# A recurrent layer, a banded attention and a routed FFN in one launch: layer norms by rows, and the router's mask by replacing the two largest logits

## The reference, cut to what matters

```python
h = tok(x)                         # 16 sequences, 375 rows of 128; z, f, o from a 2-tap convolution,
                                   # c = f*c + (1-f)*z along the rows, h = o*c: 374 rows of 128
h = h + attention(layernorm(h))    # 8 heads; each row looks back at 33 near offsets (0..32)
                                   # and at 48, 64, 96, 128, 192, 256; gated; then W_out, b_out
h = h + ffn(layernorm(h))          # logits over 64 experts, top 2, softmax weights,
                                   # at most 128 rows per expert, one shared GELU FFN (512 wide)
def layernorm(x): return (x - mean(x)) / sqrt(var(x) + 1e-5)    # over the 128 channels of a row
```

## Time and profile before

| | |
|---|---|
| median of 3 runs | 496.3 us (495.8 to 497.25) |
| the profiled execution's own time | 499.14 us |
| its span, first to last instruction | 497.3 us |
| mean granted clock of TensorE | 0.991 of full |
| h of sequence 0 and of sequence 15 made at (L831) | 11.3 and 405.3 us |

### The profile page before, as it was taken

One profiled execution on the slowest core, in us unless ns is written; L12 is line 12 of the kernel. 1 busy time (PEld: TensorE's weight loads), 2 busy tenths in 40 slices (PEclk: granted clock), 3 DMA queues, 4 the chain that ended last, 5 costly groups with the idle time before them and its releaser, 6 DMA issues.

```text
span 497.3 us, 12720 instructions
## 1 busy us (share of the span) xinstructions
PE 473.4 (95%) x4698; PEld 298.6 (60%) x4698; DVE 404.3 (81%) x837; ACT 303.0 (61%) x539; POOL 396.5 (80%) x444
## 2 busy tenths in 40 slices
PE   7689799999999999999999999999999999999994
PEld 5334446465665666666566556656655666658673
DVE  3678797888888898888789788888978889878764
ACT  4456566665765756566475657657555665747664
POOL 6299989997987879698878969878796988986511
PEclk9799999999999999999999999999999999999999
DMA  6000539080724417081542707145180633535901
GB/s 246 15 1 1 132 62 190 11 181 2 180 28 115 94 58 150 2 192 16 129 79 57 151 1 181 27 112 97 52 157 1 164 45 94 100 96 97 192 18 31
DMA packets 54222, 44.27 MB, mean 89 GB/s; under 512 B 27248, under 2 KB 41488, under 8 KB 54032
## 3 DMA queue, kind: packets, MB, share of 16 engines
q1 hardware_dynamic: 54160, 43.45, 39.5%
HBM read 24.59 MB, written 18.85 MB: 87 GB/s over the span
## 4 chain that ended last, share of the span: by engine, by line
PE 79%; DVE 6%; POOL 5%; issue 4%; DMA 4%; ACT 2%; SPq 1%; POOLq 0%; DVEq 0%; ACTq 0%
PE bank L367 19%; PE bank L353 8%; PE bank L462 7%; PE bank L485 6%; PE bank L332 6%; PE bank L333 5%; PE bank L430 4%; PE bank L417 3%; PE bank L341 2%; PE bank L346 2%; PE bank L409 2%; PE bank L381 2%; PE bank L437 2%; PE bank L442 2%; PE bank L447 2%
## 5 line engine op out<-in xcount | busy, mean ns | idle before, releaser
L1140 POOL TENSOR_TENSOR prod<-q,k 128x1496 f32<-128x1496 f32 x48 | 144.0, 3014 | 13.3 <-ACT q L630 13.3
L850 DVE SCALAR_TENSOR_TENSOR prod<-bank,par,k 128x1496 f32<-128x1496 f32 x80 | 139.5, 1768 | 7.5 <-ACT q L630 7.5
L1182 POOL TENSOR_TENSOR acc<-acc,tmp 128x310 f32<-128x310 f32 (+4 forms) x80 | 64.8, 810 | 38.4 <-DVE tmp L907 24.1
L367 PE MATMUL bank<-prod,ew 128*32 128x374 f32 x1024 | 90.3, 481 | 0.8 <-DVE mixin L817 0.8
L1125 POOL TENSOR_TENSOR fprod<-q,k 128x374 f32<-128x374 f32 (+6 forms) x112 | 80.2, 746 | 0.0
L654 ACT ACTIVATE scT<-bank 128x374 f32<-128x374 f32 x48 | 23.2, 484 | 64.8 <-PE bank L367 64.8
L353 PE MATMUL bank<-xn,par 128*128 128x374 f32 x128 | 53.7, 506 | 2.9 <-DVE xn L839 2.9
L485 PEld LDWEIGHTS bank<-par,hid 128*128 128x128 f32 x384 | 47.6, 191 | 9.9 <-issue 6.8
L367 PEld LDWEIGHTS bank<-prod,ew 128*32 128x32 f32 x1024 | 28.9, 110 | 37.6 <-issue 34.7
L485 PE MATMUL bank<-par,hid 128*128 128x128 f32 x384 | 50.1, 275 | 0.9 <-ACT hid L713 0.9
L907 DVE TENSOR_TENSOR tmp<-bank,vT 128x310 f32<-128x310 f32 (+4 forms) x80 | 30.3, 380 | 23.9 <-PE bank L409 22.2
(11 more groups left out here) (130 smaller groups left out, 977.4 us busy)
## 6 DMA issues: line engine op xcount, KB each, us to landing
band_scratch<-attn SPq DMA_DIRECT2D x16, 769.5 KB, 6.0
band<-band_scratch SPq DMA_DIRECT2D x64, 192.0 KB, 3.8
v<-v_scratch SPq DMA_DIRECT2D x32, 192.0 KB, 5.0
v_scratch<-vtok SPq DMA_DIRECT2D x16, 192.0 KB, 4.1
xT<-x_dram SPq DMA_DIRECT2D x16, 187.5 KB, 4.2
out_dram<-osb SPq DMA_DIRECT2D x16, 128.0 KB
par<-params_dram SPq DMA_DIRECT2D x1, 1819.5 KB, 7.7
out_dram<-osb SPq DMA_DIRECT2D x16, 59.0 KB
```

Source lines behind the costliest of these rows:

```text
L367: done = mm(home(f"s{c}")[32 * g:32 * g + 32, 0:N], ew[:, c * CW + j, :], src[:, j, :], start=first or only, stop=last or only)
L850: v.scalar_tensor_tensor(bass.AP(prod[c][:, :, :].tensor, part * N, [[CW * N, 128], [PARTS * N, w], [1, N]]), home("q")[:, 0:N].unsqueeze( ...
L1140: g.tensor_tensor(bass.AP(prod[c][:, :, :].tensor, part * N, [[CW * N, 128], [PARTS * N, w], [1, N]]), q[q_.s][:, :].unsqueeze(1).broadcas ...
L1182: g.tensor_tensor(acc[:, o:N], acc[:, o:N], tmp[i % 2][:, o:N], ALU.add).then_inc(acc_added[i], 1)
```

## The change

1. **First layer norm by rows.** `turn_h` turns h (three 128x128 transposes), `stats1` on VectorE takes mean and variance of each row (three BN_STATS, three BN_AGGR), ScalarE makes the reciprocal root of 128x3 elements, `shift_rows` makes minus mean times it (128x3), `norm1_rows` normalises (three 128x128), `turn_x` turns back (three transposes), `norm1_back` copies to xn. `keep_rows` keeps the turned h, and `carry` on GpSimd adds the output bias to it.
2. **Second layer norm by rows.** `out_project` makes rows directly (three matmuls of 128 columns for one of 374), so h2 is in rows from the start: `stats2`, `norm2_ln`, `norm2_exp`, `shift2_rows`, `norm2_rows`, `turn_x2`, `norm2_back` are as above. `turn_h2` goes, and `finish` reads h2 itself.
3. **Router's mask.** The two largest logits are copied, MATCH_REPLACE puts another value in their places, and the mask is where the result differs from the logits.
4. **Scores.** The far sums are turned with three transposes into a bank of their own, and `score_add` has three calls of one piece. The far offsets stand in another order (96, 48, 128, 64, 192, 256), and the second step of their sums leaves out the first 96 columns.
5. **Order and banks.** Every `turn` is written anew, with new banks. TensorE's and VectorE's a0 is empty: a sequence now goes through five turns of TensorE. ScalarE's turn loads a table four times, not two.

The new order of each turn (the digit is the place in the pipeline):

- TensorE: logits 5, up[3] 5, up[2] 5, turn_scores[0] 3, score[1] 3 (four steps), turn_x 2, spread_far[3] 4, turn_band[1] 4, turn_scores[1] 3, spread_far[4] 4, project k and q 2, turn_band[0] 4, spread_far[5] 4, turn_band[2] 4, convolve z 1, attend[0] 4, up[1] 5, project gate 3, attend[1], attend[2] 4, convolve o 1, up[0] 5, positions 5, out_project 4, convolve f 1, down[0] 5, project v 2, far_weights 3, down[1] 5, score[2] first step, score[0] (four), score[2] second step 2, turn_h 1, turn_x2 4, spread_far[1], [0] 3, turn_values 2, down[2] 5, spread_far[2] 3, turn_scores[2] 2.
- VectorE: two products 2, softmax_sum 3, attention_sum 4, softmax_rcp 3, attention_gate 4, softmax_gain and softmax_out 3, keep 5, residual 4, take_room 5, a product 2, stats2 4, recur_in 1, a product 2, shift2_rows 4, recur 1, weight_sum 5, recur_out 1, a product 2, far_value[1] 3, gate_sum 5, far_value[0] 3, stats1 1, gate_weight and add_b2 5, score_add[2] 2, finish 5, shift_rows 1, route_max 4, score_add[0] 2, route_picks 4, far_value[2] 3, route_mask 4, far_value[3] 3, score_add[1] 2, far_value[4] 3, score_max 2, far_value[5] 3.
- ScalarE (its a0 is the others' a1): band_copy[0] 3, table ln/exp, softmax_exp 2, band_copy[2] 3, table gelu, tanh_gate 2, tanh_z 0, gelu[1], gelu[0] 4, tanh_o 0, keep_rows 1, tanh_f and half_forget 0, table ln/exp, norm2_ln 3, copy_v 1, norm2_exp 3, router_exp 4, far_copy 2, norm2_rows 3, score_copy[0], [2] 1, norm2_back 3, value_rows 1, norm1_ln and norm1_exp 0, logit_copy 3, table gelu, gelu[3] 3, norm1_rows 0, score_copy[1] 1, norm1_back 0, gelu[2] 3, band_copy[1] 2, copy_k and copy_q 0.
- GpSimd (its a0 is the others' a2): far_sum[5] 2, far_products[0] 0, far_attention and split_far 1, kept_mask 3, far_products[1] 0, a product 0, kept_weights 3, two products 0, far_sum[1] 1, router_subtract 2, far_sum[2], [3] 1, score_subtract 0, far_sum[4] 1, carry 1.

The core of the diff (the second norm's functions differ from the first's in names and tiles; the turns stand above):

```diff
-            def center(q_, *before):
+            def turn_h(q_, *before):
                 if is_first(q_):
                     pe.wait_ge(par_in, 32)
+                    pe.wait_ge(pads_zero, 1)
                 freed(pe, before)
                 pe.wait_ge(h_ready, q_.b + 1)
-                mm(home("hc")[:, 0:N], P("cen4"), h[q_.s][:, :], start=True, stop=True).then_inc(hc_mm, 1)
...
-                freed(pe, before)
-                pe.wait_ge(sq_ready, q_.b + 1)
-                mm(home("var")[:, 0:N], P("avg"), stat[:, :], start=True, stop=True).then_inc(var_mm, 1)
+                for t in range(TT):
+                    done = tr(home("ht")[:, t * 128:(t + 1) * 128], h[q_.s][:, t * 128:(t + 1) * 128], ident)
+                done.then_inc(h_turned, 1)
+
+            def turn_x(q_, *before):
+                freed(pe, before)
+                pe.wait_ge(xrow_ready, q_.b + 1)
+                for t in range(TT):
+                    done = tr(home("xb")[:, t * 128:(t + 1) * 128], xrow[:, t, :], ident)
+                done.then_inc(x_turned, 1)
 
...
+                lo = SHORT if c == CH and not first else 0
                 for g in range(CG):
                     j = n * g + r
                     if j < end:
                         only = c == CH and g == CG - 1
-                        done = mm(home(f"s{c}")[32 * g:32 * g + 32, 0:N], ew[:, c * CW + j, :], src[:, j, :],
+                        done = mm(home(f"s{c}")[32 * g:32 * g + 32, lo:N], ew[:, c * CW + j, :], src[:, j, lo:N],
...
-                pe.wait_ge(scT_ready[CH], q_.b + 1)
-                pick_rows = bass.AP(par[:, :].tensor, COL["ident"][0], [[PCOLS, 128], [32, CG], [8, LSTEPS], [1, 8]])
-                width = CG * LSTEPS * 8
-                dst = home(f"ts{c}")
-                for t in range(TT):
-                    tr(dst[:, t * 128:(t + 1) * 128], scT[:, c, t * 128:(t + 1) * 128], ident)
-                for n, t in enumerate(FAR_TILES[c]):
-                    at_ = TT * 128 + n * width
-                    done = mm(dst[:, at_:at_ + width], scT[:, CH, t * 128:(t + 1) * 128], pick_rows, start=True, stop=True)
+                for t in range(TT):
+                    done = tr(home(f"ts{c}")[:, t * 128:(t + 1) * 128], scT[:, c, t * 128:(t + 1) * 128], ident)
                 done.then_inc(ts_mm[c], 1)
 
...
                 pe.wait_ge(ao_ready, q_.b + 1)
-                mm(home("op")[:, 0:N], P("outw"), ao[:, :], start=True, stop=True).then_inc(out_mm, 1)
-
...
+                act.wait_ge(stat_ready, q_.b + 1)
+                after(act, shift_ready, q_.b)
+                A(rstd[:, :], stat[:, :, 1], ACT.Ln, bias=eps16[:, 0:1]).then_inc(rstd_ready, 1)
...
+            def norm1_rows(q_):
+                act.wait_ge(shift_ready, q_.b + 1)
+                after(act, x_turned, q_.b)
+                for t in range(TT):
+                    done = A(xrow[:, t, :], home("ht")[:, t * 128:(t + 1) * 128], ACT.Identity,
+                             bias=shift[:, t:t + 1], scale=rstd[:, t:t + 1])
+                done.then_inc(xrow_ready, 1)
+
+            def keep_rows(q_):
+                act.wait_ge(part_ready, q_.b + 1)
+                after(act, h2_ready, q_.b - 1)
+                A(hkeep[q_.s][:, :, :], home("ht")[:, 0:TT * D].rearrange("p (t d) -> p t d", d=D), ACT.Copy, scale=-0.25)\
+                    .then_inc(hrow_ready, 1)
+
+            def norm1_back(q_):
+                act.wait_ge(x_turned, q_.b + 1)
+                after(act, gate_mm, q_.b - 1)
+                A(xn[q_.s][:, :], home("xb")[:, 0:N], ACT.Copy, scale=-1.0).then_inc(xn_ready, 1)
 
...
+            def norm2_back(q_):
+                act.wait_ge(x2_turned, q_.b + 1)
+                after(act, up_mm[0], q_.b)
+                after(act, logit_mm, q_.b)
+                A(x2[:, 0:N], home("x2b")[:, 0:N], ACT.Copy).then_inc(x2_ready, 1)
 
...
-            def norm1(q_):
-                dve.wait_ge(rstd_ready, q_.b + 1)
-                after(dve, v_mm, q_.b - 1)
-                v.tensor_tensor(xn[q_.s][:, :], home("hc")[:, 0:N], stat[:, :], ALU.mult).then_inc(xn_ready, 1)
+            def stats1(q_):
+                dve.wait_ge(h_turned, q_.b + 1)
+                for t in range(TT):
+                    done = v.bn_stats(part[:, t, :], home("ht")[:, t * 128:(t + 1) * 128])
+                done.then_inc(part_ready, 1)
+                dve.wait_ge(part_ready, q_.b + 1)
+                after(dve, rstd_ready, 2 * q_.b)
+                for t in range(TT):
+                    done = v.bn_aggr(stat[:, t, :], part[:, t, :])
+                done.then_inc(stat_ready, 1)
+
+            def shift_rows(q_):
+                dve.wait_ge(rstd_ready, 2 * (q_.b + 1))
+                after(dve, xrow_ready, q_.b)
+                v.scalar_tensor_tensor(shift[:, :], stat[:, :, 0], -1.0, rstd[:, :], ALU.mult, ALU.mult)\
+                    .then_inc(shift_ready, 1)
 
...
-                after(dve, h2_turned, q_.b - 1)
-                v.scalar_tensor_tensor(h2[q_.s][:, 0:N], home("op")[:, 0:N], P("bias", BOUT, BOUT + 1), hkeep[q_.s][:, :],
-                                       ALU.add, ALU.add).then_inc(h2_ready, 1)
-
-            def norm2(q_):
-                dve.wait_ge(rstd2_ready, q_.b + 1)
-                after(dve, up_mm[0], q_.b)
-                after(dve, logit_mm, q_.b)
-                v.tensor_tensor(x2[:, 0:N], home("hc2")[:, 0:N], stat2[:, :], ALU.mult).then_inc(x2_ready, 1)
+                after(dve, xrow2_ready, q_.b - 1)
+                v.tensor_tensor(h2[q_.s][:, :, :], home("op")[:, 0:TT * D].rearrange("p (t d) -> p t d", d=D),
...
                 dve.wait_ge(m8_ready, q_.b + 1)
-                for t in range(TT):
-                    last = v.max_index(i8[:, t, :], m8[:, t, :], lg[:, t, :])
-                last.then_inc(i8_ready, 1)
-
-            pairs_at, hit_at = TT * EXPERTS, TT * EXPERTS + 8
...
-                dve.wait_ge(i8_ready, q_.b + 1)
-                idf = home("lg")[:, pairs_at:pairs_at + TT * TOPK].rearrange("p (t k) -> p t k", k=TOPK)
-                v.tensor_copy(idf, i8[:, :, 0:TOPK]).then_inc(idf_ready, 1)
-
-            def route_hits(q_):
-                dve.wait_ge(idf_ready, q_.b + 1)
-                iota = P("iota").unsqueeze(1).broadcast_to([128, TT, EXPERTS])
-                idf = home("lg")[:, pairs_at:pairs_at + TT * TOPK].rearrange("p (t k) -> p t k", k=TOPK)
-                eq0 = home("lg")[:, hit_at:hit_at + TT * EXPERTS].rearrange("p (t e) -> p t e", e=EXPERTS)
-                v.tensor_tensor(eq0, iota, idf[:, :, 0:1].broadcast_to([128, TT, EXPERTS]), ALU.is_equal)
-                v.tensor_tensor(eq1[:, :, :], iota, idf[:, :, 1:2].broadcast_to([128, TT, EXPERTS]), ALU.is_equal)\
-                    .then_inc(eq_ready, 1)
+                v.tensor_copy(top[:, :, 0:TOPK], m8[:, :, 0:TOPK]).then_inc(top_ready, 1)
+                dve.wait_ge(top_ready, q_.b + 1)
+                for t in range(TT):
+                    at_ = hit_at + t * hit_width
+                    last = v.match_replace(home("lg")[:, at_:at_ + hit_width], top[:, t, :], lg[:, t, 0:hit_width], TAKEN)
+                last.then_inc(hits_ready, 1)
 
             def route_mask(q_):
-                dve.wait_ge(eq_ready, q_.b + 1)
+                dve.wait_ge(hits_ready, q_.b + 1)
                 after(dve, pos_mm, q_.b)
                 after(dve, kept2_ready, q_.b)
-                eq0 = home("lg")[:, hit_at:hit_at + TT * EXPERTS].rearrange("p (t e) -> p t e", e=EXPERTS)
-                v.tensor_tensor(msk[:, :, :], eq0, eq1[:, :, :], ALU.add).then_inc(msk_ready, 1)
+                taken = home("lg")[:, hit_at:hit_at + TT * hit_width].rearrange("p (t e) -> p t e", e=hit_width)
+                v.tensor_tensor(msk[:, :, :], taken[:, :, 0:EXPERTS], lg[:, :, 0:EXPERTS], ALU.not_equal)\
+                    .then_inc(msk_ready, 1)
...
+                dve.wait_ge(down_mm, TT * (q_.b + 1))
+                rows = home("dn")[:, 0:TT * D].rearrange("p (t d) -> p t d", d=D)
+                v.tensor_tensor(rows, rows, P("b2").unsqueeze(1).broadcast_to([128, TT, D]), ALU.add).then_inc(y1_ready, 1)
...
-                    last = v.scalar_tensor_tensor(osb[q_.s][:, t, :], y1[:, t, :], gt[:, t:t + 1],
-                                                  home("th")[:, t * D:(t + 1) * D], ALU.mult, ALU.add)
+                    last = v.scalar_tensor_tensor(osb[q_.s][:, t, :], home("dn")[:, t * D:(t + 1) * D], gt[:, t:t + 1],
+                                                  h2[q_.s][:, t, :], ALU.mult, ALU.add)
                 last.then_inc(out_ready, 1)
...
-                    .then_inc(hkeep_ready, 1)
+                pool.wait_ge(hrow_ready, q_.b + 1)
+                g.tensor_tensor(hkeep[q_.s][:, :, :], hkeep[q_.s][:, :, :], P("bo").unsqueeze(1).broadcast_to([128, TT, D]),
+                                ALU.add).then_inc(hkeep_ready, 1)
```

(11 more changed lines are left out.)

654 lines of the change are left out of this document (328 added, 326 removed).

## The result

The changed kernel takes 529.1 us (four runs, 526.3 to 529.8) where the kernel before, run beside it on the same chip, takes 496.8 (four runs, 495.8 to 498.7): ratio 1.062, 95% interval 1.059 to 1.066. Forecast were 462.4 us and "faster". The profiled execution took 528.94 for a span of 526.9.

What follows compares the result with a forecast made beforehand. TensorE's list was taken to bound a full turn: 16 x 26.3 = 420.8 us, plus 9.6 of waits and 33 for the ends, gave a span of 463.4 and a time of 462.4 us, range 451 to 481.

Steps and rivals of the forecast that it cites:

- The two shifts: 0.22 each: VectorE's list: shift_rows and shift2_rows, both new, would cost 0.22 us each in a turn.
- GpSimd: ... the shorter instructions on other engines do not touch it: GpSimd's list: same products and sums, staying at 24.3 us of a 26.3 us turn.
- VectorE's bounds, 24.3 to 27.0: VectorE's work in a full turn would go from 24.7 to 25.4 us, with these bounds.
- VectorE or its loop as the bound: Rival: at upper costs for BN_STATS and MATCH_REPLACE, list 27.0 and loop 27.2 set a 28.2 us turn; 479 us; chance 0.17.
- The prices of the new instructions: VectorE's list: both norms' statistics 2.2 us a turn, picks 1.0, third score_add 0.3; ScalarE's list 21.6.
- TensorE's floor: Full turns: TensorE's list would shorten by 2.2 us, from 28.5 to 26.3, good to about 0.2.
- The loop q, k, products, shift: Full turns: VectorE's first product to shift_rows, then back through k and q, 23.7 to 25.6 us, under 26.3.
- the slower rival with loads on the loop: Rival: three table loads on ScalarE, 3.8 us, would lengthen the loop to 29.5; median 503 us; chance 0.05.
- The ends: 33, with bounds 25 and 42: Pipeline filling and emptying: 35.0 us before, less some 3.5 for one part-filled turn, about 1.5 more for the norm's chain.
- ends well over 42: Sign of a wrong forecast: the norm's longer chain would count where the pipeline fills.
- Twelve full turns: Sum: with five TensorE turns a sequence instead of six, twelve turns are full, each with 0.8 us of waits, 9.6 together.
- GpSimd's loop: Rival: GpSimd's waits for softmax_gain and score_max, 3 to 5 us, make a turn 27.9 to 29.8; 482 to 500 us; chance 0.07.

Runs made afterwards that it cites:

- E2: Changed kernel with both norm shifts and the gate's product gt as one-column operations with a per-partition scalar: 491.4 us, ratio 0.9925 to the kernel before.
- E4: Kernel before with only the router's new mask (copy of the two largest, MATCH_REPLACE, comparison): 497.8 us, ratio 1.0049.
- E5: E2 with VectorE's one-time set-up moved behind the first norm's first shift: 487.3 us, ratio 0.983 to the kernel before.
- E9: The same edit as E5, run again on another chip: 486.4 us, ratio 0.979 to the kernel before.
- E10: The same edit as E8, run again on the same chip as E9: 485.5 us, ratio 0.979 to the kernel before.
- E6: E5 with the recurrence behind two products, not four, and two table loads left out while the pipeline fills: 490.8 us, ratio 0.990 to the kernel before.
- E12: E5 with q and k ahead of the previous sequence's scores, and GpSimd's first far products earlier, while filling: 503.4 us, ratio 1.016 to the kernel before.
- E8: E5 with 6, 7 and 8 dummy matmuls in three places where TensorE stands while filling: 485.8 us, ratio 0.976 to the kernel before.
- E3: Changed kernel with the GpSimd product that shift2_rows meets issued as two halves: 519.2 us, one run.

## Why the prediction was wrong

The sign was wrong through one term of the sum, the size of the gain through a second. Step by step:

- **"The two shifts: 0.22 each" is the step that failed.** It took the duration of L998, the nearest row by size (128x3) and by operands (two SBUF tensors), and missed that this duration depends on GpSimd. The trace of before held the sign. In its full turns L998 came 0.66 us into a far product of 0.87 and ended 19 ns behind it, at 0.24 us; where GpSimd was idle it took 0.16:

```profile
212.41 0.87 POOL L1125 TENSOR_TENSOR fprod<-q,k 128x326 f32<-128x326 f32 x1
...
213.07 0.23 DVE L998 TENSOR_TENSOR gt<-gs,rcr 128x3 f32<-128x3 f32 x1
...
484.54 0.16 DVE L998 TENSOR_TENSOR gt<-gs,rcr 128x3 f32<-128x3 f32 x1
```

  The forecast should have asked what GpSimd runs at the place where `shift2_rows` was put, the middle of a product. It measured 2.36 us on average and 2.6 in the full turns. Taken away (E2) it and its two like are worth 37.5 us of the 63.5 that the span was over the forecast's 463.4. This alone turns the sign: 463.4 + 37.5 = 500.9, over the 497.3 of before.
- **"GpSimd: ... the shorter instructions on other engines do not touch it"** is true of its busy time in all (24.3 forecast, 24.5), though not of every row (last section), and was the wrong question. The Trainium skill (SBUF — State Buffer, "SBUF: two separate sides") says that VectorE and GpSimd share a pair of SBUF ports as "an **exclusive lock**, not a bandwidth split", held for the whole instruction, and names VectorE's operations with two SBUF inputs among those that take it. The trace agrees: 2.59 us for three elements a partition, ended 0.02 us after GpSimd's product. The forecast weighed another page and not this one. It speaks against exactly this change.
- **VectorE's bounds, 24.3 to 27.0, left it out.** VectorE shows 27.6 busy a turn. The rival nearest to what happened, VectorE or its loop as the bound, had a chance of 0.17 and gave 479: its mechanism (unmeasured new instructions too dear) is not what happened either. BN_STATS, BN_AGGR and MATCH_REPLACE came in as forecast.
- **The prices of the new instructions were right.** Both norms' statistics (10.8 + 10.7 + 5.0 + 5.0) / 16 = 1.97 us a turn, forecast 2.2. Picks (10.0 + 4.1 + 3.3) / 16 = 1.09, forecast 1.0. The third score_add 0.31, forecast 0.3. ScalarE 21.8, forecast 21.6. Only the copy among the picks has the same flaw as the shifts: 0.21 us in the kernel after, up to 0.94 elsewhere (E4).
- **TensorE's floor was right:** 26.3 forecast, 26.67 with TensorE busy 100% of eleven turns (E2). That VectorE's 25.7 stays under it was right too. The loop q, k, products, shift, forecast at 23.7 to 25.6, doesn't set the turn in E2. Whether the loop or VectorE's list (27.6 of 29.18) set it in the kernel after was not isolated: `shift2_rows` lies on both.
- **The table loads were right:** four a turn at 1283 ns. This is how the kernel after has them (groups of ScalarE):

```profile
L727 ACT ACT_TABLE_LOAD x20 | 25.7, 1283 | 3.8 <-DVE hbias L799 3.5
L732 ACT ACT_TABLE_LOAD x20 | 25.7, 1283 | 0.3
L747 ACT ACT_TABLE_LOAD x20 | 25.7, 1283 | 0.4
L772 ACT ACT_TABLE_LOAD x20 | 25.7, 1283 | 0.4
```

  So the slower rival with loads on the loop (0.05, median 503) did not happen. The drain of some 1380 ns that the Trainium skill (ScalarE: Activation LUTs, "What ACT_TABLE_LOAD costs") adds isn't in these rows.
- **"The ends: 33, with bounds 25 and 42" was half of what they are.** They are 74.4 in the kernel after; without the port's waits 64.5 (E2), and with the set-up moved 61 (E5: 487.1 - 294.3 for the full turns - 131.5 = 61.3). The step took the idle time of before and subtracted a turn's share. But the ends' length hardly moved, 206.0 before and 196.0 in E2, while the work in them fell from six turns (171.0) to five (131.5). TensorE's idle time in them rose from 21.8 (13.1 and 8.7) to 42.1 (21.4 and 20.7). The prediction named "ends well over 42" as a sign that the norm's longer chain counts where the pipeline fills. In part it does. These are TensorE's longest waits up to the h of sequence 4 in E2:

```profile
PE bank L356 <- ACT xrow L612: 8.4, 2, 8.3
PE bank L403 <- POOL far L1213: 5.7, 2, 4.4
PE bank L349 <- DVE h L849: 3.1, 1, 3.1
```

  For the first sequence's normalised rows TensorE stands once for 8.3 us (4.2 in E5); before, its longest wait for the norm there was 2.9. The steps from h to h while it fills are 23.5, 20.5, 28.2 and 26.2 us in E2, the last two about as long as a full turn, and were 15.0, 17.5, 21.5, 22.7 and 26.1 before. That the chain of one sequence through its steps sets the ends as a whole is argued, not shown.
- **Twelve full turns** were counted; from h to h, as the ten of before were, there are eleven. At 0.8 a turn that is nothing.
- **A rival's sum** doesn't come out: GpSimd's loop at 27.9 a turn gives 462.4 + 12 x 0.8 = 472, not 482. It did not happen, and nothing else rests on it.

With the two terms put right the sum closes: 420.8 + 11 x 0.37 + 64.5 = 489.4, the span of E2.

**What stays open** is which waits make the ends 61 and not 33. The set-up accounted for some 4 us (E5, E9). The clock is excluded while the pipeline fills (E9 against E10), not while it empties: from the h of sequence 15 on, E9 took 86.9 us at 0.93 and E10 85.2 at 0.97. Two other orders for the filling turns made it worse (E6, E12), which shows that the order there is tightly bound, and not by what. The best version that was run is E5's, 0.979 to 0.983 of the kernel before; E8's, with dummy matmuls, can't be told from it. The copy of six elements still waits in it (866 ns in the mean); taking it off that port wasn't tried.

## What to carry to other kernels

The duration of a small VectorE instruction holds only for its operands and for what GpSimd runs beside it: before pricing one with two SBUF inputs, or an fp32 copy within SBUF, look up in GpSimd's timeline what stands at its place, and add the rest of that instruction. Where GpSimd runs instructions of microseconds, small products on VectorE go as operations over one column with a per-partition scalar, or with one operand in PSUM; wider ones with a scalar can wait too (last section). Halving GpSimd's instruction only passed the wait to the next of its kind (E3).

A sequence's stay in the pipeline became a turn shorter, and the ends still gave back only 10 us (206.0 to 196.0), where the work in them fell by 39.5 (171.0 to 131.5). Before pricing the ends by work, follow the first sequence's chain through them: 5 us of set-up taken off it gave four (E5).
